# Moving work between the engines of a masked-attention kernel: two bounds and the end's work to VectorE, sums copied out as one product, one subtraction per block put later

## The reference

```python
scores = leaky_relu(x @ ks.T, 0.2)
scores = where(adj > 0, scores, -9e15)
attn   = softmax(scores, axis=1)
y      = x + attn @ ks
out    = (y - mean(y)) / sqrt(var(y) + 1e-5)     # per row
```

## Time and profile before

| what | value |
|---|---|
| median of 3 runs (lowest, highest) | 1552.17 us (1549.71, 1552.98) |
| the profiled execution's own time | 1553.51 us |
| its span, first to last instruction | 1551.4 us |
| mean granted TensorE clock | 0.994 |
| busy over the span: PE, PEld, DVE, ACT, POOL | 97%, 92%, 97%, 95%, 93% |
| chain that ended last: PE, issue, DVE, ACT, POOL | 70%, 11%, 9%, 7%, 3% |
| DMA | 191 GB/s mean |

### The profile page before, as it was taken

How to read it: one execution, slowest core, us unless ns; L and a number is a source line. 1 busy time by engine, 2 the same in 40 slices (tenths; PEclk the granted TensorE clock), 3 DMA queues, 4 the chain that set the end, 5 groups by cost and what they waited for, 6 DMA issues and landing times.

```text
span 1551.4 us, 43381 instructions
## 1 busy us (share of the span) xinstructions
PE 1509.1 (97%) x16828; PEld 1419.9 (92%) x16828; DVE 1501.4 (97%) x1808; ACT 1480.0 (95%) x1887; POOL 1440.4 (93%) x1246
## 2 busy tenths in 40 slices
PE   6699999999999999999999999999999999999997
PEld 5499999999999999999999999999999999999987
DVE  6999999999999999999999999999999999999984
ACT  6999999999999999999999999999999999999997
POOL 4999999999999999999999999999999999999996
PEclk8999999999999999999999999999999999999999
DMA  9865656555556655566665555655655655555610
GB/s 352 271 200 191 197 198 203 196 188 195 194 191 190 202 189 196 192 191 196 199 192 191 188 188 188 200 183 188 194 189 189 201 185 189 193 188 189 197 63 8
DMA packets 107131, 296.00 MB, mean 191 GB/s; under 512 B 10800, under 2 KB 40240, under 8 KB 106928
## 3 DMA queue, kind: packets, MB, share of 16 engines
q1 hardware_dynamic: 106928, 293.25, 57.6%
HBM read 289.01 MB, written 4.19 MB: 189 GB/s over the span
## 4 chain that ended last, share of the span: by engine, by line
PE 70%; issue 11%; DVE 9%; ACT 7%; POOL 3%; DVEq 0%; DMA 0%; ACTq 0%; POOLq 0%
PE weighted L806 20%; PE scores L758 10%; PE scores L760 10%; PE scores L759 10%; PE weighted L822 6%; PE weighted L818 6%; PE weighted L820 6%; DVE ring L680 3%; ACT ring L493 3%; DVE running L664 3%; ACT pt_hi L500 2%; DVE ring L650 1%; POOL pt_lo L401 1%; POOL kt_lo L363 1%; ACT xt_hi L468 1%
## 5 line engine op out<-in xcount | busy, mean ns | idle before, releaser
L396 POOL TENSOR_TENSOR ring<-ring,floor 128x768 f32<-128x768 f32 (+1 forms) x498 | 706.2, 1418 | 49.2 <-ACT floor L520 49.2
L401 POOL TENSOR_TENSOR pt_lo<-ring,pt_hi 128x512 f16<-128x512 f32 (+1 forms) x512 | 659.5, 1288 | 17.7 <-ACT pt_hi L500 17.2
L650 DVE SCALAR_TENSOR_TENSOR ring<-adj_sb,scores 128x1024 f32<-128x1024 int32 x512 | 620.2, 1211 | 6.8 <-ACT scores L486 6.4
L486 ACT ACTIVATE scores<-scores,shrink 128x1024 f32<-128x1024 f32 x512 | 553.8, 1082 | 51.5 <-PE scores L760 47.0
L493 ACT ACTIVATE ring<-ring,lift 128x1024 f32<-128x1024 f32 x512 | 583.6, 1140 | 1.6 <-POOL ring L396 1.2
L758 PE MATMUL scores<-xt_hi,kt_hi 128*128 128x256 f16 x2048 | 559.8, 273 | 22.8 <-DVE ring L650 15.2
L760 PE MATMUL scores<-xt_hi,kt_lo 128*128 128x256 f16 x2048 | 560.4, 274 | 0.0
L759 PE MATMUL scores<-xt_lo,kt_hi 128*128 128x256 f16 x2048 | 560.1, 273 | 0.0
L664 DVE TENSOR_TENSOR running<-ring,running 128x1024 f32<-128x1024 f32 x448 | 547.2, 1221 | 0.1
L806 PE MATMUL weighted<-k_rows,ring 128*128 128x129 f32 x3472 | 471.6, 276 | 2.0 <-DVE y L701 1.0
L806 PEld LDWEIGHTS weighted<-k_rows,ring 128*128 128x128 f32 x3472 | 426.6, 192 | 14.1 <-ACT ring L493 8.2
(11 more groups left out here) (76 smaller groups left out, 559.2 us busy)
## 6 DMA issues: line engine op xcount, KB each, us to landing
adj_sb<-in_adj SPq DMA_DIRECT2D x512, 512.0 KB, 3.4
ring<-in_ks_t SPq DMA_DIRECT2D x8, 512.0 KB, 7.3
x_row<-in_x SPq DMA_DIRECT2D x32, 128.0 KB, 3.6
out<-normed SPq DMA_DIRECT2D x32, 128.0 KB, 3.6
x_probe<-in_x_t SPq DMA_DIRECT2D x29, 128.0 KB, 3.5
xt_raw<-in_x_t SPq DMA_DIRECT2D x29, 128.0 KB, 4.4
ring<-in_ks SPq DMA_DIRECT2D x12, 128.0 KB, 7.4
k_rows<-in_ks SPq DMA_DIRECT2D x12, 128.0 KB, 3.8
```

What stands on the lines that cost most here:

```text
L396: nc.gpsimd.tensor_tensor(here, here, below, ALU.subtract).then_inc(gap_ready, 1)
L401: nc.gpsimd.tensor_tensor(pt_lo[:, g % PARTS, 0:QUAD - whole, :], ring[:, g % RING, whole:, :], pt_hi[:, g % PARTS, 0:QUAD - whole, :], AL ...
L650: nc.vector.scalar_tensor_tensor(ring[:, g % RING, :, :], adj_sb[:, g % ADJS, :, :], 0.0, scores[:, g % 2, :, :], ALU.is_le, ALU.subtract)\
```

## The change

- Start: steps 6 and 7 of the bounds of ks_t go from ScalarE to VectorE (ahead of the masks of slots 4 and 5). ScalarE's splits of ks_t go one slot earlier, and its bound of step 4 goes from slot 1 to slot 3, that of step 5 from slot 3 to slot 5.
- `finish` is cut in two: reciprocal of the sums' last column, then one product of 128x256 from PSUM to `ratio` in SBUF, which frees the bank; `residual` (the scaling by `unscale` and the addition of x) comes at the end of the slot. `denom` goes. In that slot the early `gap` stands ahead of `finish`.
- The subtraction of a block's group 15 is no longer early. It is done at delay 19. Counted by the block b whose `spread` waits for it, it stands in VectorE's slot 16b+18, between `mask` and the first `least` of that block, where it stood in slot 16b+17.
- End: VectorE takes all tiles of the subtraction in the last 18 groups (three tiles in the two before). It waits for `spread` itself in block 31, and ScalarE's copy of the minimum goes there. VectorE does `high_part` of the last 8 groups and `normalise` of block 31, and GpSimd's `shift` goes for that block.

```diff
-    MAGNITUDES = (2, 4, 6, 7, 8, 9)
+    MAGNITUDES = (2, 4, 8, 9, 10, 11)
-    LEFT_OUT = GROUPS - 2
+    LEFT_OUT = GROUPS + 2
+    LAST_HIGHS = 8
...
-            return QUAD if g >= ALL - LEFT_OUT else 3 if g >= ALL - GROUPS else min(1 + g % 4, 2)
+            return QUAD if g >= ALL - LEFT_OUT else 3 if g >= ALL - LEFT_OUT - 2 else min(1 + g % 4, 2)
+        def wait_high(eng, g):
+            if g < ALL - LAST_HIGHS:
+                eng.wait_ge(part_hi_ready, g + 1)
+            else:
+                eng.wait_ge(dve_hi_ready, g + 1 - (ALL - LAST_HIGHS))
...
 # ScalarE
-                if g is not None:
+                if g is not None and g < ALL - LAST_HIGHS:
                     high_part(g)
...
-                if 3 <= s < 6:
-                    bound_ks_t(s + 2, s)
-                if s < 8:
+                if s == 0:
+                    split_ks_t(2)
+                if s == 5:
+                    bound_ks_t(5, 3)
+                elif s < 5:
+                    split_ks_t(s + 3)
+                elif s < 8:
                     split_ks_t(s + 2)
-                if s == 1:
+                if s == 3:
                     bound_ks_t(4, 2)
...
 # VectorE
-                dve.wait_ge(floor_ready, b + 1)
+                if b == BLOCKS - 1:
+                    dve.wait_ge(spread_ready, b + 1)
+                else:
+                    dve.wait_ge(floor_ready, b + 1)
...
             def finish(b):
-                nc.vector.tensor_scalar(denom[:, :], total[:, :, ONES], scale_rows, None, ALU.mult).then_inc(denom_ready, 1)
-                dve.wait_ge(denom_ready, b + 1)
+                nc.vector.reciprocal(recip[:, :], total[:, :, ONES]).then_inc(recip_ready, 1)
+                dve.wait_ge(recip_ready, b + 1)
                 wait(dve, y_ready, SIDES * b)
-                nc.vector.reciprocal(recip[:, :], denom[:, :]).then_inc(recip_ready, 1)
+                nc.vector.tensor_tensor(ratio[:, :, :], total[:, :, 0:D],
+                                        recip[:, :].unsqueeze(2).to_broadcast([P, SIDES, D]), ALU.mult)\
+                    .then_inc(ratio_ready, 1)
+            def residual(b):
+                dve.wait_ge(ratio_ready, b + 1)
                 dve.wait_ge(xrow_loaded[at], 16 * (b // 2 + 1))
-                dve.wait_ge(recip_ready, b + 1)
                 wait(dve, normed_ready, SIDES * b)
                 for j in range(SIDES):
-                    nc.vector.scalar_tensor_tensor(y[:, j, :], total[:, j, 0:D], recip[:, j:j + 1],
-                                                   x_row[:, at, j, :], ALU.mult, ALU.add,
-                                                   accum_out=y_sum[:, j:j + 1]).then_inc(y_ready, 1)
+                    nc.vector.scalar_tensor_tensor(y[:, j, :], ratio[:, j, :], unscale_rows, x_row[:, at, j, :],
+                                                   ALU.mult, ALU.add, accum_out=y_sum[:, j:j + 1]).then_inc(y_ready, 1)
+            def high_part(g):
+                dve.wait_ge(prob_ready, g + 1)
+                dve.wait_ge(weighted_ready, g + 1 - PARTS)
+                whole = WHOLE[g % GROUPS]
+                nc.vector.tensor_copy(pt_hi[:, g % PARTS, 0:QUAD - whole, :], ring[:, g % RING, whole:, :])\
+                    .then_inc(dve_hi_ready, 1)
+            def normalise(b):
+                dve.wait_ge(rstd_ready, b + 1)
+                for j in range(SIDES):
+                    nc.vector.tensor_scalar(normed[:, b % 2, j, :], y[:, j, :], neg_mean[:, j:j + 1], rstd[:, j:j + 1],
+                                            ALU.add, ALU.mult).then_inc(normed_ready, 1)
             for s in SLOTS:
-                b = whole(s, AT_FINISH)
-                if b is not None:
-                    finish(b)
+                if 4 <= s < 6:
+                    dve.wait_ge(ks_t_loaded[s + 2], 16)
+                    magnitude(mag_k[:, s + 2:s + 3], ks_t_raw[:, (s + 2) * STEP:(s + 3) * STEP])
                 if s == 6:
                     most(2)
+                ended = whole(s, AT_FINISH)
+                if ended is not None:
+                    if ended < BLOCKS - 1:
+                        gap(s - AT_GAP + 1)
+                    finish(ended)
+                    if ended == BLOCKS - 1:
+                        residual(ended)
                 g = group(s, 0)
                 if g is not None:
                     mask(g)
+                g = group(s, AT_PART)
+                if g is not None and g >= ALL - LAST_HIGHS:
+                    high_part(g)
...
                 for early in (False, True):
                     g = group(s, AT_GAP - 1 if early else AT_GAP)
-                    if g is not None and early == (g % GROUPS > 0):
+                    if g is not None and early == (0 < g % GROUPS < LAST) and (ended is None or ended == BLOCKS - 1):
                         gap(g)
                 g = group(s, 1)
                 if g is not None and 0 < g % GROUPS < LAST:
                     least(g)
+                if ended is not None and ended < BLOCKS - 1:
+                    residual(ended)
 # TensorE, weigh
-                    wait(pe, y_ready, SIDES * b)
+                    wait(pe, ratio_ready, b)
```

More of the change, by code:

```diff
@@ L100, in adj_attention_layernorm @@
         lift = sb("lift", [P, 1], F32)
-        denom = sb("denom", [P, SIDES], F32)
+        ratio = sb("ratio", [P, SIDES, D], F32)
         xt_raw = sb("xt_raw", [P, 3, BLOCK], F32)
@@ L173, in adj_attention_layernorm @@
         dve_gap_ready = sem("dve_gap_ready")
+        dve_hi_ready = sem("dve_hi_ready")
         part_hi_ready = sem("part_hi_ready")
         part_lo_ready = sem("part_lo_ready")
-        denom_ready = sem("denom_ready")
+        ratio_ready = sem("ratio_ready")
         prob_ready = sem("prob_ready")
@@ L230, in adj_attention_layernorm @@
         scale_rows = f32_column(scale, K_ALL)
+        unscale_rows = f32_column(unscale, K_ALL)
         def scales_there(stage):
@@ L398, in low_part @@
             def low_part(g):
-                pool.wait_ge(part_hi_ready, g + 1)
+                wait_high(pool, g)
                 whole = WHOLE[g % GROUPS]
@@ L415, in deviation @@
                 nc.gpsimd.tensor_tensor(rstd[:, :], var[:, :], minus_half[:, :], ALU.pow).then_inc(rstd_ready, 1)
+                if b == BLOCKS - 1:
+                    return
                 pool.wait_ge(rstd_ready, b + 1)
@@ L561, in _ @@
                         bound_x(b)
-                b = whole_late(s, AT_SPREAD, 1)
-                if b is not None:
+                b = whole(s, AT_SPREAD)
+                if b is not None and b < BLOCKS - 1:
                     spread(b)
@@ L689, in finish @@
             def finish(b):
-                at = b % 2
                 total = sums(b)[:, 0:SIDES * LANES].rearrange("p (j w) -> p j w", j=SIDES)
                 dve.wait_ge(weighted_ready, GROUPS * (b + 1))
-                nc.vector.tensor_scalar(denom[:, :], total[:, :, ONES], scale_rows, None, ALU.mult).then_inc(denom_ready, 1)
-                dve.wait_ge(denom_ready, b + 1)
+                wait(dve, ratio_ready, b)
+                nc.vector.reciprocal(recip[:, :], total[:, :, ONES]).then_inc(recip_ready, 1)
@@ L695, in finish @@
+                dve.wait_ge(recip_ready, b + 1)
                 wait(dve, y_ready, SIDES * b)
-                nc.vector.reciprocal(recip[:, :], denom[:, :]).then_inc(recip_ready, 1)
+                nc.vector.tensor_tensor(ratio[:, :, :], total[:, :, 0:D],
+                                        recip[:, :].unsqueeze(2).to_broadcast([P, SIDES, D]), ALU.mult)\
+                    .then_inc(ratio_ready, 1)
+            def residual(b):
+                at = b % 2
+                dve.wait_ge(ratio_ready, b + 1)
@@ new lines, in high_part @@
+            def high_part(g):
[5 more added lines that the diff above has]
+            def normalise(b):
+                dve.wait_ge(normed_ready, SIDES * b)
+                dve.wait_ge(out_stored[b % 2], 16 * (b // 2))
+                dve.wait_ge(rstd_ready, b + 1)
+                for j in range(SIDES):
+                    nc.vector.tensor_scalar(normed[:, b % 2, j, :], y[:, j, :], neg_mean[:, j:j + 1], rstd[:, j:j + 1],
+                                            ALU.add, ALU.mult).then_inc(normed_ready, 1)
@@ L713, in _ @@
                     mask(g)
+                g = group(s, AT_PART)
+                if g is not None and g >= ALL - LAST_HIGHS:
+                    high_part(g)
+                if whole(s, AT_NORMALISE[0]) == BLOCKS - 1:
+                    normalise(BLOCKS - 1)
                 if s == 0:
@@ L716, in _ @@
                 if s == 5:
-                    dve.wait_ge(mag_k_bounded, 6)
+                    dve.wait_ge(mag_k_bounded, 4)
+                    dve.wait_ge(mag_step, 6)
                     magnitude(mag[:, K_SETS[2]:K_SETS[2] + 1], mag_k[:, CUTS[2]:CUTS[3]])
@@ L808, in weigh @@
                                          start=(q == t == j == 0), stop=False, skip_group_check=True)
```

(2 more changed lines are left out.)

1 line of the change is left out of this document (removed).

## The result

The changed kernel takes 1559.61 us (median of 5 runs, 1557.68 to 1559.73), the kernel before, beside it, 1550.76 us (5 runs, 1549.71 to 1552.98). The ratio is 1.0046, 95% interval 1.0035 to 1.0058: about 0.5% slower, some 7 to 9 us. The forecast was 1553.9, so the sign of its sum (+1.7) was right and its size too small. The measured time lies at the upper edge of the stated range, 1541.5 to 1559.5 (by the ratio, 1552.17 becomes 1559.3), and outside the forecast's own one (1550.5 to 1557). The profiled execution took 1557.68 us, span 1555.8 (before 1553.51 and 1551.4).

The account below looks back on a forecast made before the run. TensorE and VectorE were both taken to be within 0.3 us of the pace, so moved waits decide. Start -1.6, middle +7.2 and end -3.9 gave +1.7 us on the median 1552.17: 1553.9, range 1541.5 to 1559.5.

Parts of the forecast that it names:

- a product of 0.55 us: Rival in `finish`: the product from PSUM costs what two `y` cost, 0.55 us, giving 1560.3 us; chance 0.13.
- The end of a block: In `finish`: the product takes 0.33 us, the bank is free earlier, and TensorE's 0.28 us of idle go.
- The moved subtraction: Group 15's subtraction, now behind slot 2's mask, makes `spread` wait: TensorE gains 0.28 us, then stands for 0.51.
- The ring: From a block's sums through mask, subtraction and `spread` to the next sums: 46.71 us, against 46.48 now.
- Nothing else on VectorE fills this: Behind the waiting `spread`, VectorE has nothing else to do and waits about 0.3 us per block.
- +6.7: Middle of the run: 29 periods, each 0.23 us longer, cost 6.7 us.
- rival 1: Middle: the moved subtraction doesn't hold TensorE, VectorE's 46.31 us is the pace, giving 1541.4 us; chance 0.25.
- New-scale blocks: Two middle blocks where VectorE makes new scales between the sums and the subtraction: +0.5 us together.
- +7.2: Whole middle: 6.7 us for 29 longer periods plus 0.5 for two blocks with new scales.
- The start: Kernel start: `most(2)` runs 2.3 us earlier, at 29.65, leaving -1.6 us at the first sums.
- Rival 3: Kernel start: it gives nothing since GpSimd's low parts set it, giving 1556.2 us; chance 0.07.
- The end: Last blocks: last sums 3.5 us earlier and 0.4 saved behind them, -3.9 us in all.

Follow-up runs that it names:

- run 3: Changed kernel with GpSimd's low part of each block's group 13 cut to 8 columns: 1555.73 us, ratio 1.0022.
- run 2: Kernel before with only the subtraction of group 15 moved behind the mask of slot 2: 1569.55 us, ratio 1.0113.
- run 6: Changed kernel with the subtraction of group 15 early again and GpSimd's low part of group 13 cut to 8 columns: 1539.93 us, ratio 0.9928.
- run 1: Changed kernel with the subtraction of group 15 early again, all else kept: 1552.47 us, ratio 1.0005.
- run 4: Changed kernel with the subtraction of group 15 still later, behind the first minimum: 1647.76 us, ratio 1.0619.
- run 8: Kernel before with only the change's end (subtractions, high parts and `normalise` on VectorE): 1548.30 us, ratio 0.9982.
- run 9: Kernel before with the change's end and a scaled ones column replacing `denom`, `y` still reading PSUM, subtraction not moved: 1537.83 us, ratio 0.9918.
- run 5: Changed kernel with the subtraction of group 15 early again and GpSimd's mean put behind its subtraction in the slot: 1577.51 us, ratio 1.0172.

## Why the prediction was right in sign and short in size

The number owes something to luck. The range reached up towards a product of 0.55 us and a start that gives nothing. The product took 0.34. What the forecast lacked, beside the start, were the blocks with new scales and the seven late blocks, which no rival had. The outcome held for likeliest, no difference that the runs can tell (0.42), didn't come; slower had been given 0.30, of which the product had 0.13.

**The end of a block: right.** The product was put at 0.33 us and takes 0.34; its recorded mean is 424 ns, near the 411 of the row that it was taken from the earlier trace rows. TensorE's 0.28 us of idle go.

**The moved subtraction: right.** The ring was put at 46.71 us and is 46.68 (the changed kernel, and run 3). By the same working it was put at 46.97 for the move alone, and is 47.00 (run 2). From the subtraction to `spread` it took 0.83 us, as in the row of before, 0.82.

**"Nothing else on VectorE fills this: ... VectorE will wait there for about 0.3 us": wrong.** This is the step that failed. The first minimum fills those 0.3 us: it takes 1.60 us instead of 1.22, because GpSimd's low part runs 0.5 us into it. Take the low part away and the wait of 0.3 us is there (run 3). In typical blocks the long minimum is hidden under the ring, so the forecast of +6.7 for them is near the measured +5.8 for the right reason. But it takes the slack away. Where the ring isn't the bound, as in the forecast's rival 1, VectorE would go at 46.31 by my sum, does go at 46.24 with the low part cut short (run 6, 1539.93 us), and goes at 46.63 with it (run 1): that rival's 1541.4 was never to be had from putting the subtraction back alone.

**New-scale blocks: a term mis-sized, +0.5 put, +3.8 measured.** The scales' work on VectorE ends in `shrink`, which took 0.55 us in the same block before (343.36 to 343.91, where a low part ended at 343.88), and takes 0.28 where that low part is cut short (run 3). VectorE, then GpSimd, then TensorE of the changed kernel:

```profile
342.12 1.21 DVE L627 TENSOR_SCALAR shrink<-unscale 128x3 f32<-128x3 f32 x1
...
351.30 1.22 DVE L666 SCALAR_TENSOR_TENSOR ring<-adj_sb,scores 128x1024 f32<-128x1024 int32 x1 [1.91 <-ACT scores L498]
```

```profile
342.17 1.15 POOL L411 TENSOR_TENSOR pt_lo<-ring,pt_hi 128x512 f16<-128x512 f32 x1
```

```profile
345.20 0.40 PE L845 MATMUL floors<-eye,low 128*128 128x128 f32 x2 [2.43 <-DVE ring L699]
```

`shrink` ends at 343.33, with GpSimd's instruction (342.17 + 1.15 = 343.32), so the subtraction behind it is late, `spread` waits 2.43 us, and ScalarE's queue hands 1.91 of it to the mask, as in run 4. The other block with new scales is as late at `spread` (2.24 us) but loses nothing in the queue, hence 48.86 and not 50.70. With that low part short, 3.5 us come back (run 3). These 3.3 us above the term and the seven late blocks (+1.9, not forecast), less the 0.9 by which typical blocks stay below +6.7, are the difference between +7.2 and +11.5.

**The start: wrong.** `most(2)` was put at 29.65 and runs at 30.06 where it stood at 31.98, and the first sums came 3.0 us earlier in that trace. But with the old start other traces have `most(2)` at 30.28 to 30.63 (runs 2, 8 and 9), and with the new one it lies between 29.85 and 31.18. Mask 8 is at 36.94 and 37.63 (runs 2 and 8), where the row of before has 39.68, and with the new start between 36.65 and 39.08. TensorE's granted clock differs with it. Windows of the kernel before, then of run 2 with the same start (the third last number is the clock):

```profile
25.00:30.00 5.00, 3.51 (x17) 2.19 (x16) 3.88 (x6) 3.96 (x7) 2.07 (x3) 0.50 1.06 390
30.00:37.00 7.00, 4.79 (x28) 3.50 (x26) 5.41 (x11) 4.14 (x5) 4.52 (x6) 0.74 0.81 285
```

```profile
25.00:30.00 5.00, 2.56 (x25) 2.12 (x22) 4.36 (x6) 3.96 (x8) 2.88 (x4) 1.00 1.06 391
30.00:37.00 7.00, 3.80 (x33) 2.85 (x32) 5.80 (x11) 5.15 (x7) 5.21 (x7) 1.00 1.03 364
```

The kernel before had the lower of the clock's two levels (1.2 GHz) throughout the first of these stretches, and run 2 had the upper one (2.4 GHz) in both. The row that I read was one draw from a spread of 3 us. Rival 3 was right here, and cost me 1.6.

**The end: right in size.** -3.9 put, -4.1 in the traces of the changed kernel and of run 8, and -2.8 by the runs of the latter. The copies on VectorE were priced from the earlier trace rows, with the figure of the Trainium skill beside it. VectorE of the kernel after:

```profile
1535.72 0.48 DVE L734 CAST pt_hi<-ring 128x512 f16<-128x512 f32 x1
1536.12 1.21 DVE L699 TENSOR_TENSOR ring<-ring,floors 128x1024 f32<-128x1024 f32 x1
...
1542.67 1.26 DVE L734 CAST pt_hi<-ring 128x512 f16<-128x512 f32 x1 [1.15 <-PE scores L878]
```

A free copy takes 0.40 us from start to start, between the 0.60 that I took and the 0.33 that was estimated from the Trainium skill, "VectorE: DVE Perf Modes", section "The perf-mode tier table". The last one shown starts while GpSimd runs three low parts (until 1539.47 + 4.19 = 1543.66) and ends 0.27 behind them.

**The mechanism behind the failed step.** In each case above a VectorE instruction ended no sooner than GpSimd's running one, and each time it read two operands from SBUF (first minimum, `y` from `ratio`) or was a copy or scaling of one SBUF tensor (`pt_hi`, `shrink`). The 448 other minima, with one operand in PSUM, keep 1221 ns beside a GpSimd that is busy 92% of the time. The Trainium skill, "SBUF — State Buffer", section "Who interferes with whom", states a rule that fits: a VectorE instruction with two SBUF inputs contends with a GpSimd instruction that reads SBUF, one in a 2-port mode with any, and the later of the two waits for the whole of the earlier. The traces agree for the first minimum (1.60 = 0.51 of waiting + 1.09, and 1.09 behind the low part in all 81 such blocks of the changed kernel and runs 1 and 4). Which of two is the later one can't always be read from the records: `shrink` is recorded as starting 0.05 us ahead of the low part that it ends with. The change turned `y` into an instruction of this kind, and moved both the low part (0.4 us later after the sums) and the first minimum (0.3 us earlier). The forecast left GpSimd's place at nothing and looked at neither.

**Left open.** What makes VectorE late at the subtraction in six blocks of the first half. That GpSimd's 0.93 us of waiting for `y` is what puts the low part 0.4 us later is likely (in most blocks the low part starts 35.2 us after the sums with the late `y`, and 34.6 to 34.8 in the kernel before and in runs 2 and 9), but run 5, which was to show it, moved the first minimum as well. Why run 9 gains 2.6 us more than its sum isn't settled either; in its trace the end is 4.6 us shorter, not 4.1, and the first sums come 3.6 us earlier. Letting `spread` go ahead of the last subtraction was not tried: both halves of `floors` share a bank, and the subtraction would still be reading it.

## What to carry to other kernels

When several engines are within 1% of the pace, work out every ring that passes through a moved step, by starts; that part of the forecast held to 0.03 us a block. Then ask of each VectorE instruction with two operands in SBUF, or copying within it, what GpSimd does at that time, and of each step that you delay, which GpSimd instruction waits for it: that shifts what lies over what. Rather than free a bank faster by copying it, look for an operation that can be folded into data made once: here a scaled ones column took 0.26 us out of each block and moved nothing (-0.8% with the end).

## What the runs showed of the hardware that I had not expected

- A VectorE instruction of 128x128 took 1.63 us instead of 0.35 because GpSimd had started a 1.81 us instruction 0.33 us before it (run 5). The lock works the other way too: GpSimd's subtraction of 128x768 that starts under the first minimum in run 1 is recorded with 2.09 us; the one in the row of the kernel after, which starts only 0.15 us ahead of the minimum's end, with 1.84.
- The same kernel start, in different executions, has the mask of slot 8 anywhere from 36.9 to 39.7 us, with the granted clock of TensorE between 1.00 and 0.74 from 30 to 37 us: a start can't be compared from two traces.
- A product of PSUM with a scalar stretched over 128 elements costs what a plain operation of that size costs (0.34 us for 256 elements from start to start).
